# Attention scores from full-height matmuls in a gated cross-attention and feed-forward kernel

## What is computed

```python
q, k, v = proj(layernorm(x), Wq, bq), proj(ctx, Wk, bk), proj(ctx, Wv, bv)   # 16 heads of 32
scores = clip(einsum('bhsd,bhtd->bhst', q, k) / sqrt(32), -50, 50)            # masked to -50
delta = softmax(scores) @ v @ Wo.T + bo        # then scaled and layer-normed
x = x + tanh(g_xattn) * delta
h = silu(bit_linear(layernorm(x), gate_w, gate_b)) * bit_linear(layernorm(x), val_w, val_b)
x = x + tanh(g_ffn) * bit_linear(h, out_w, out_b)
# bit_linear: x rounded to 8-bit codes by token, w to -1, 0, 1
```

## Time and profile before

| | |
|---|---|
| median of three runs (lowest, highest) | 741.14 us (740.9, 741.32) |
| the profiled execution's own time | 740.9 us |
| its span, first to last instruction | 739.1 us |
| PE busy | 689.7 us, 93% |
| DVE busy | 592.5 us, 80% |
| ACT busy | 505.7 us, 68% |
| POOL busy | 311.6 us, 42% |
| mean granted clock of TensorE | 0.974 of full |

### The profile page before, as it was taken

How to read it: one execution, slowest core, us unless ns; L and a number is a source line. 1 busy time by engine, 2 the same in 40 slices (tenths; PEclk the granted TensorE clock), 3 DMA queues, 4 the chain that set the end, 5 groups by cost and what they waited for, 6 DMA issues and landing times.

```text
span 739.1 us, 13613 instructions
## 1 busy us (share of the span) xinstructions
PE 689.7 (93%) x4333; PEld 331.5 (45%) x4333; DVE 592.5 (80%) x1243; ACT 505.7 (68%) x668; POOL 311.6 (42%) x482
## 2 busy tenths in 40 slices
PE   4999657779999999999999999999999999999996
PEld 4435435344544354445444544444444444444443
DVE  6896698488787988888887888788878877778865
ACT  4485778689657866786578767786679656855563
POOL 4310315223654356435734474446534643354530
PEclk9999885999999999999999999999999999999999
DMA  8874525312653266335443544336433632263213
GB/s 330 246 243 151 118 90 155 102 31 56 129 132 71 70 126 127 77 85 114 107 106 85 112 101 114 85 85 128 100 74 75 149 71 56 52 129 83 56 43 72
DMA packets 170323, 80.09 MB, mean 108 GB/s; under 512 B 149496, under 2 KB 149788, under 8 KB 169647
## 3 DMA queue, kind: packets, MB, share of 16 engines
q1 hardware_dynamic: 170286, 79.64, 44.5%
HBM read 37.85 MB, written 10.56 MB: 66 GB/s over the span
## 4 chain that ended last, share of the span: by engine, by line
PE 77%; DVE 9%; ACT 5%; DMA 4%; issue 3%; POOL 0%; SPq 0%; DVEq 0%; ACTq 0%
PE psum L1747 26%; PE psum L1781 22%; PE psum L1772 13%; PE psum L1845 5%; PE psum L1824 3%; PE psum L1751 2%; DMA arena<-in_L_xattn_Wq 2%; DMA extra<-in_L_ffn_out_w 1%; PE psum L1739 1%; PE psum L2001 1%; ACT arena L913 1%; PE psum L1988 1%; PE psum L1759 1%; DVE hmax L1259 1%; PE psum L1700 1%
## 5 line engine op out<-in xcount | busy, mean ns | idle before, releaser
L1747 PE MATMUL psum<-ternary,xqT 128*128 128x512 f16 x1024 | 246.3, 381 | 1.5 <-ACT arena L873 1.5
L1747 PEld LDWEIGHTS psum<-ternary,xqT 128*128 128x128 f16 x1024 | 96.1, 98 | 119.3 <-issue 9.3
L1772 PE MATMUL psum<-ternary,arena 128*128 128x512 f16 x496 | 116.1, 379 | 2.9 <-DMA arena<-arena 2.9
L680 POOL TENSOR_TENSOR rstd<-var_e,minus_half 128x1 f32<-128x1 f32 x64 | 39.8, 622 | 182.4 <-DVE var_e L1297 92.4
L873 ACT ACTIVATE arena<-psum,dequant 128x512 f32<-128x512 f32 x128 | 86.2, 679 | 40.8 <-PE psum L1751 26.6
L881 ACT ACTIVATE arena<-arena,round_c,hscale 128x1024 f32<-128x1024 f32 x62 | 73.7, 1239 | 15.1 <-DVE hscale L1271 15.1
L1781 PE MATMUL psum<-wo_hi,arena 128*128 128x512 f16 x256 | 81.4, 379 | 0.0
L1259 DVE TENSOR_REDUCE hmax<-arena 128x1 f32<-128x1024 f32 x64 | 77.5, 1211 | 0.5
L1781 PE MATMUL psum<-arena,wq_hi 128*128 128x512 f16 x256 | 77.2, 383 | 0.2
L1254 DVE SCALAR_TENSOR_TENSOR arena<-psum,dequant,arena 128x512 f32<-128x512 f32 x80 | 59.5, 745 | 17.9 <-ACT arena L873 15.6
L1772 PEld LDWEIGHTS psum<-ternary,arena 128*128 128x128 f16 x496 | 45.8, 98 | 59.9 <-issue 10.5
(11 more groups left out here) (216 smaller groups left out, 1233.4 us busy)
## 6 DMA issues: line engine op xcount, KB each, us to landing
arena<-in_x SPq DMA_DIRECT2D x64, 256.0 KB, 2.8
out<-arena SPq DMA_DIRECT2D x31, 256.0 KB, 2.3
arena<-in_L_ffn_gate_w SPq DMA_DIRECT2D x4, 1024.0 KB, 12.9
arena<-in_L_ffn_out_w SPq DMA_DIRECT2D x3, 1024.0 KB, 4.9
ternary<-in_L_ffn_val_w SPq DMA_DIRECT2D x2, 1024.0 KB, 11.2
arena<-arena SPq DMA_TRANSPOSE x90, 3.1
ternary<-in_ctx SPq DMA_DIRECT2D x1, 1024.0 KB, 5.5
ternary<-in_L_xattn_Wk SPq DMA_DIRECT2D x1, 1024.0 KB, 8.0
```

Of the source, the lines that this page charges most:

```text
L1747: ins = M.matmul(ps[:], xqT[:, t % 2, k, :], w[:, k, cols], start=(i >= 2 and k == 0), stop=(k == KC - 1 and not last_bias))
L1772: ins = M.matmul(psO[:], hidT[t % 2][:, k, :], wo2[:, k, :], start=(k == 0), stop=(k == FC - 1))
```

## The change

The scores of a pair of heads come from matmuls over all 128 partitions.

- `q_parts` holds for each pair j the high part of its query on the 64 partitions where it was computed, and the low part on the other 64. ScalarE's cast becomes two, each on 64 partitions; `q_low` becomes two subtractions on 64 partitions, each of which writes to the other half.
- `kcur` holds each pair's keys on both halves, so it is twice as large, and `load_keys` issues eight DMAs of 32 KB instead of four.
- A pair's scores are two matmuls: high keys with the high and low query stacked, then low keys with the same. That is 16 in a row of x. The product low x low is now included.
- Score banks: `psA[1]`, `psA[0]`, `psG[0]`, `psG[1]` in turn in the loop (`psV[0]` is no longer used), and the two `psA` alone in the first row, where there were four.
- The waits are set by pair. The projection in t = 1 waits for the sixth exponential instead of the third.
- `down` is cut into other pieces around the scores: 6, 2, 2, 2 matmuls after pairs 3, 4, 5, 6, and the last four behind `xq_transpose`.
- The value bias of chunk (1, 3) is added by TensorE; VectorE adds five in a body in place of six.

```diff
-        q_parts = room(6).bitcast(F16).rearrange("p (two m s) -> p two m s", two=2, m=KC)
+        q_parts = room(6).bitcast(F16).rearrange("p (j s) -> p j s", j=NPAIR)
...
-            return (psA[1], psA[0], psO, psT)[j % 4] if row is FIRST + 1 else (psA[1], psG[0], psA[0], psG[1], psA[1], psG[0], psV[0], psG[1])[j]
+            return psA[(j + 1) % 2] if row is FIRST + 1 else (psA[1], psA[0], psG[0], psG[1])[j % 4]
...
         def biased_by_vector(t, n):
-            return t != 2 and n >= 2
+            return t in (0, 3) and n >= 2 or (t, n) == (1, 2)
...
                 for i in range(HPC):
-                    e = i % 2
-                    head = slice(HD * i, HD * (i + 1))
-                    sp.dma_start(kcur[head, :, e * T:(e + 1) * T], keys[head, :, row, :]).then_inc(k_loaded.sem, 16)
+                    for q in range(2):
+                        e = i % 2
+                        head = HD * (2 * q + e)
+                        sp.dma_start(kcur[HD * i:HD * (i + 1), q::2, e * T:(e + 1) * T],
+                                     keys[head:head + HD, :, row, :]).then_inc(k_loaded.sem, 16)
...
-                    A.copy(q_parts[:, 0, m, :], whole).then_inc(qh_ready.sem, 1)
+                    A.copy(q_parts[0:P // 2, 2 * m, :], whole[0:P // 2, :])
+                    A.copy(q_parts[P // 2:, 2 * m + 1, :], whole[P // 2:, :]).then_inc(qh_ready.sem, 1)
...
-                V.tensor_tensor(q_parts[:, 1, m, :], q_whole[:, m % 2, :], q_parts[:, 0, m, :],
+                one, other = slice(0, P // 2), slice(P // 2, P)
+                whole = q_whole[:, m % 2, :]
+                V.tensor_tensor(q_parts[other, 2 * m, :], whole[one, :], q_parts[one, 2 * m, :], ALU.subtract)
+                V.tensor_tensor(q_parts[one, 2 * m + 1, :], whole[other, :], q_parts[other, 2 * m + 1, :],
                                 ALU.subtract).then_inc(ql_ready.sem, 1)
...
-                    terms = ((0, 0), (0, 1), (1, 0))
-                    for n, (k_part, q_part) in enumerate(terms):
-                        for h in range(2):
-                            pair = slice(h * P // 2, (h + 1) * P // 2)
-                            ins = M.matmul(score_bank(a, 2 * m + h)[:], kcur[pair, k_part * KC + m, :],
-                                           q_parts[pair, q_part, m, :], start=(n == 0), stop=(n == len(terms) - 1))
+                    if j == 1:
                         wait(pe, d_ready, b, 3)
+                    if b is FIRST and j >= 2:
+                        wait(pe, p_ready, a, j - 1)
+                    elif j in (2, 3):
+                        wait(pe, silu_done, b, NCH + j + 1)
+                    elif j > 3:
+                        wait(pe, p_ready, a, j - 3)
+                    ps = score_bank(a, j)
+                    M.matmul(ps[:], kcur[:, j, :], q_parts[:, j, :], start=True, stop=False)
+                    M.matmul(ps[:], kcur[:, NPAIR + j, :], q_parts[:, j, :],
+                             start=False, stop=True).then_inc(sc_done.sem, 1)
...
-                        wait(pe, p_ready, a, 3)
+                        wait(pe, p_ready, a, NPAIR - 2)
...
-BETWEEN_SCORES = {1: range(0, 10), 2: range(10, 16)}
-AFTER_SCORES = 16
+BETWEEN_SCORES = {3: range(0, 6), 4: range(6, 8), 5: range(8, 10), 6: range(10, 12)}
+AFTER_SCORES = 12
```

More of the change, by code:

```diff
@@ L1876, in first_row @@
                     largest_to_all(4)
-                    for m in range(KC):
-                        scores(m)
+                    for j in range(NPAIR):
+                        scores(j)
                     weighted(0)
```

37 lines of the change are left out of this document (12 added, 25 removed).

## The result

The changed kernel takes 747.57 us (median of 12 runs, 742.45 to 750.85) where the kernel before took 740.9 in the same sessions. The ratio is 1.0087, with a 95% interval of 1.0063 to 1.011: slower by 4.7 to 8.1 us. The forecast of 747.2 was right. Several of its terms were not, and they cancelled.

What follows compares the result with a forecast made beforehand. TensorE bounds the loop; before it, a chain of ScalarE, VectorE and DMAs does. Terms 2.6 + 0.2 + 1.1 + 2.2 = 6.1 us on 740.9 give 747.0, or 747.2 at the median; range 744.2 to 751.2.

Steps and rivals of the forecast that it cites:

- The loop: Bodies 1 to 6: full-height scores and the bias slot cost +0.22 us each a row, +2.6 us in all.
- It saves VectorE 0.75 us, which buys nothing in the loop: Bias term: moving chunk (1, 3) costs TensorE one slot, +0.22 us; VectorE's saved 0.75 us gains nothing in the TensorE-bound loop.
- the score banks ... I cost this at nothing: New score order in the loop: waits for exponentials met with 0.9 us or more to spare, banks free sooner; cost nothing.
- cover too thin: Rival, in the loop: late subtractions or hidden codes use up the cover; 0.4 us in each of seven bodies gives 750; chance 0.14.
- The price of the halves: Split query copies: each half takes the old full duration, +0.52 us on ScalarE and +0.60 on VectorE per query chunk.
- The first row: Before the loop: scores +1.15 us, exponentials start +0.5 and take +0.4 to +0.5 from two banks; weighted sums +1.1 us.
- The clock case: Rival, first row: TensorE's clock stays at 2.4 GHz instead of falling, some 2.3 us come back: 744.9; chance 0.13.
- What is late here stays late: First row to first body: VectorE, 17.90 of 20 us busy from 107 on, hardly pauses, so the first row's delay persists.
- The keys' DMAs: Eight key DMAs instead of four: 3 us more on SP's queue, covered by 1.4 us or more at the transposes; nothing.
- Body 0: Before the loop: split casts and subtractions delay `delta` and the output-weight transposes by 1.0 + 1.2 = +2.2 us.
- Body 0's pass: Body 0's scores cost +0.2 us; idle time of 0.48 us ahead of them takes in the bias slot.
- body 7: No scores there, and TensorE's 0.30 us wait for a DMA transpose behind chunk (1, 3) takes in the bias slot: nothing.

Runs made afterwards that it cites:

- Value bias back: The changed kernel with the value bias of chunk (1, 3) added by VectorE again: 753.73 us, 1.0193 to the kernel before.
- Only the split: The kernel before with only the query casts and subtractions in halves of 64 partitions, each on its own partitions: 749.72 us, 1.0151.

## Why the prediction came out right, and where it was wrong

**The loop: +0.43 us a pass, predicted 0.44.** The scores' and the bias's slots each have their 0.22, and nothing else is late, if only just: VectorE's idle time ahead of the statistics of t = 1 is 0.10 us, where it was 0.57 before and is 1.73 with no split. But two sentences behind the sum were wrong. "It saves VectorE 0.75 us, which buys nothing in the loop": it buys 0.95 us a pass without the split (77.80 against 76.85) and 1.36 with it (78.20 against 76.84 or 76.85). And "the score banks ... I cost this at nothing" looked only at when the scores' own waits are met, not at what the sooner exponentials set off: ScalarE's cast, GpSimd, and VectorE's bounding beside it. The change carries a cost of about 1.2 us a pass (1.39 less the scores' 0.22) and its cure, and I had seen neither. The row that shows how little slack VectorE has is the 0.57 us before 334.66. I had looked for cover at the border from t = 0 to t = 1 (2.26 and 2.81 us), where there is plenty, and not at the next one. It is also the rival "cover too thin", true for the split alone (+0.84 a pass), with the bias slot as what keeps it away.

**The price of the halves.** I took the old start-to-start times, +0.52 and +0.60; they are +0.75 and +0.82. The rule of the Trainium skill (VectorE: DVE Perf Modes, Two Vector instructions with no wait between them), that an instruction starting in another group of 32 partitions waits for all earlier ones, is borne out on VectorE: 0.70 to 0.72 us apart in place of 0.60. (In body 0 of the changed kernel the statistics, which read PSUM, follow a half after 0.61, from 161.10 to 161.71.) ScalarE shows the same, 0.63 in place of 0.52.

**The first row: predicted +1.1 us to the weighted sums, measured +2.57** (84.26 to 88.63, less the 1.80 of this execution's setup). The last query to the scores takes 1.53 more (predicted 1.15), and the scores to the weighted sums 1.04 more (predicted: nothing, as the exponentials were to start 0.5 later and take 0.4 to 0.5 more). Runs with a granted clock of 1.00 in this stretch give the two parts that I had: the split alone takes 7.33 us from the scores to the weighted sums where the kernel before has 7.72, the new scores with their two banks 8.19, together +0.08. The other 0.96 us are the clock. It fell to 0.50, 1.2 GHz, at 78.24, in the 2.92 us of idle time ahead of the scores, and stayed there to 85.07; the score matmuls start 0.40 to 0.43 us apart until 85.00, and two banks feed at that clock. With the same instructions "Value bias back" had the low clock for half as long and took 8.24, and "Only the split", with the same idle time, kept 1.00 up to 86.31: so this part differs from one execution to the next. In turn the weighted sums run at 2.4 GHz sooner, and 0.99 us come back by the first weight transposes: +1.58 there. The clock case was half true, by another way than I had it.

**"What is late here stays late": it stayed late up to the last weight chunk.** The weight sum of body 0 stands at 137.70 before and 137.86 after. TensorE waited 4.72 us there and now 0.45. The wait ends with the last chunk of the output weights; its issue on SP's queue, before and after:

```profile
124.63 0.43 SPq L472 DMA_DIRECT2D extra<-in_L_ffn_out_w  x1
```
```profile
127.75 0.42 SPq L472 DMA_DIRECT2D extra<-in_L_ffn_out_w  x1
```

The first row's 1.58 and the setup's 1.80 are there almost whole when it is issued, 3.12 us later, and then they vanish: it lands at 135.43 and at 135.59, after 10.8 us before and after 7.8 now. No slack took the delay in; a transfer did that took 3 us less. I had read VectorE's 17.90 busy us of 20 as a chain without slack, and had not followed the wait at 137.70 to ScalarE's [1.06 <-DMA extra].

**The keys' DMAs: predicted nothing, probably a gain.** Over the profiled executions that last chunk lands 9.0 to 12.0 us after its issue in seven kernels with four key DMAs behind it on the queue (10.8 in the mean), and 7.4 to 10.4 us after it in six with eight or with all of them doubled (8.4 in the mean). The doubled keys alone made the kernel before 2.6 us faster (0.9965). In the loop the term was right; ahead of it the sum lacks a gain of that size, and a part of it is chance.

**Body 0: predicted +2.2 us, measured +1.79.** From the weight sum to the transposes of the output weights are 26.54 us (137.86 to 164.40) where there were 23.76 (137.70 to 161.46), +2.78; from there to the scores 9.59 where there were 10.58, -0.99. My 2.2 stood for the transposes, so it is the 2.78 that answers to it. VectorE's first three query chunks have the halves of 0.69 us, and the third meets GpSimd:

```profile
156.81 1.63 DVE L1231 TENSOR_TENSOR arena<-arena 64x512 f16<-64x512 f32 x1
158.45 0.69 DVE L1232 TENSOR_TENSOR arena<-arena 64x512 f16<-64x512 f32 x1
```

In the kernel before, its one subtraction took 1.75 us at 155.52, so that collision is in both. The term was right in kind and 0.6 short; at the first score the total is near the forecast because dearer halves and a shorter stretch behind them offset each other.

**Body 0's pass: +0.88, and body 7: nothing, as predicted.** In body 0 the fifth and the seventh pair of scores start 0.06 and 0.37 us later after the first score than in the loop (5.12 instead of 4.75 for the seventh), waiting for ScalarE's exponentials: there the new order has a wait of its own, which I had cost at nothing. In body 7 the bias slot fills the 0.30 us of idle time behind chunk (1, 3), as predicted: `down` stands 67.52 us after the last row's first score before and 67.90 after, and the same +0.38 is there 15 us sooner, at a wait for a DMA (52.75 and 53.13). From the first score of body 6 to the end are 109.09 us where there were 108.65, +0.44, of which 0.22 are body 6's scores.

**The sum.** In the two profiled executions the first score of body 0 is 1.95 us later, the six passes take 3.05 more (the first +0.88, five of +0.40 to +0.45) and the rest 0.44: 5.44 us. Predicted were 3.3 (1.1 + 2.2) up to the first score of body 0 and 2.8 (0.2 + 2.6) behind it. This pair of executions cannot carry the sum to the microsecond: 1.80 of its 5.44 us are the setup, 3 us were given back by one transfer, and the medians of twelve runs are 6.7 apart. What is shown is the loop, 2.6 of the 6.1 predicted; ahead of it a first row that cost more, a clock that differs between executions and a faster transfer make up the rest. That the total came within 1 us of the forecast was luck in part, as it was in the loop, where a collision that I had not seen and its cure cancel.

## What to carry to other kernels

Before calling an engine's saving worthless, look for its shortest slack at every hand-over of the pass, not at the one where the work is added: here 0.57 us at one border decided, beside 2.8 at another. When a step is made ready sooner, follow what its consumer sets off next, on all engines, for it may begin to collide. And follow each idle time ahead of a stretch to its real end, with the issue and the landing of the transfer that ends it: here the landing gave back a delay of 3 us that no slack had covered, and issuing this transfer sooner, with two borders fewer in the loop, made the kernel before 4.0 us faster.

## What the runs showed of the hardware

- Two bounding instructions of VectorE on 128x1024 take 1.28 us where both have begun when GpSimd starts, 2.25 where one has, and 3.00 to 3.35 where GpSimd is first; a lengthened one ends 0.55 us after the GpSimd instruction that it met. GpSimd's first addition takes 1.16 us, and 1.51 to 1.67 where one of the pair had 0.5 us or more to run at its start; the second takes 1.27 or 1.72.
- Casts on 64 partitions in alternating halves start 0.63 us apart on ScalarE, where full ones are followed after 0.52.
- Half-height matmuls run in pairs, 0.216 us a pair, and each change between half and full height costs about 0.1 us: two fewer saved 0.21 us a pass. The pairing held also where three of one half were issued ahead of three of the other.
- The first row's granted clock differs between executions of the same instructions: 0.50 from 78.24 to 85.07 us in the changed kernel, from 76.64 to 80.06 in "Value bias back".
- The last weight chunk lands 7.4 to 12.0 us after its issue where it stands behind the transposes of x, and 5.9 us after it where it is issued ahead of them. That more key DMAs behind it let it land sooner (8.4 instead of 10.8 us in the mean) rests on one execution of each of thirteen kernels and on the doubled keys' 0.9965; why they do is open.
